# Audio tower on one core: projection folded behind its layer norm, a new order of all slots, and 20 products without use

## Chip, core and metric

The kernel runs on one core of a Trainium2 chip. The metric is the device time of one execution in microseconds (us). Matrix products run on TensorE (PE in the profile, its weight loads PEld), element-wise work on VectorE (DVE) and ScalarE (ACT), powers and most indirect transfers on GpSimd (POOL), loads on SyncE (SP).

## What is computed

64 signals of 4000 samples go through seven one-dimensional convolutions to 128 channels, each followed by a layer norm over the channels and an exact gelu. Twelve tokens a signal remain. They are normalised, projected to 192, and pass one attention layer and a feed-forward layer with nine experts:

```
for w, g, b, s in zip(conv_ws, ln_gs, ln_bs, strides):
    h = gelu(layernorm(conv1d(h, w, s), g, b))
norm_h = layernorm(h, fln_g, fln_b)
h = norm_h @ proj_w + proj_b
h = h + attention(layernorm(h))              # 6 heads of 32, softmax over 12 tokens
x = layernorm(h); p, routes = max, argmax of softmax(x @ Ws + bs)
out[e] = gelu(x @ W1[e] + b1[e]) @ W2[e] + b2[e]
h = h + (common = out[0], mixed with out[routes] by p)
```

All of it is float32. A 128x128 or wider product is two instructions in the trace ("x12" is six products).

## The kernel before

**Groups and chunks.** The 64 signals are eight groups (g = 0 to 7) of eight. A layer of a group is cut into chunks of up to four blocks of 128 columns; chunk (l, g, k) is cut k of layer l. There are 16 chunks a group, 128 in all. A chunk runs `conv` on TensorE, a square on ScalarE (L1371), a sum on VectorE (L1090), an addition and a power on GpSimd (L601, L604), a product with the result on VectorE (L1100), a `turn` (transposition) on TensorE (L772), and the gelu on ScalarE (L1389, L1400). Its transposition comes two slots after its convolution (`LAG`), so two other convolutions lie in between. A convolution also waits until the result of three chunks earlier has been read, and a transposition until the gelu of the chunk before has emptied the one bank that both use.

**Slots.** The order of everything is the list `SLOTS`: a head of 25 slots (`HEAD`, groups 0 and 1), bodies of 16 slots for groups 2 to 6, 18 slots `LAST` for group 7, and 34 slots `DRAIN`. A slot names one convolution chunk (or none), jobs, and preparations. Every engine goes through the slots in order and does its share of each. Jobs are: `raw`, `z`, `xt` (statistics and transposition of the samples), `l0` (layer 0: one product on TensorE, one gelu of 128x512 on ScalarE), and in the drain `up` and `down` of the common expert 0 (`down` i is six products of 128x192 for the 96 tokens of group i). A preparation `pow` is a power on GpSimd over 10 to 12 columns (L595), an `xs` scales samples on VectorE. After the head, jobs share two banks.

**Token runs.** When the last layer of group r is done, its 96 tokens go through run r (r = 0 to 7), a chain of small steps, whose slots come from the tables `STEP_AT` and `TIGHT`: `turn_h` transposes the tokens, `stat_h` and `power_h` make mean and rstd, `norm_h` (VectorE) normalises, `turn_norm_h` transposes back, `affine_h` (ScalarE) applies scale and offset, `project` multiplies by the 128x192 matrix, `stat_1` adds the bias and takes statistics, and then `power_1`, `norm_1`, `turn_1`, `qkv`, `scores`, `mask`, `less_max`, `exp` (ScalarE, which loads another function table for it and the gelu's again afterwards), `turn_probs`, `values`, `turn_heads`, `out_project`, `residual`, `norm_2`, `turn_2`, `logits`, `choose`, `rank`, `slot`, `scatter`. Run 7 has nothing but jobs beside it: in its slots TensorE also does `down` 4 (before `project`), `up` jobs and `down` 5 (between `turn_heads` and `out_project`).

**End.** After the last slot TensorE does `down` 6, six `up` jobs and `down` 7, waits for them, and then runs 13 tiles of 128 tokens sorted by expert (L991 to L1015).

## Time and profile before

| | |
|---|---|
| median of 3 runs | 624.17 us (621.41 to 624.65) |
| profiled execution, its own time | 617.57 us |
| its span, first to last instruction | 615.8 us |
| TensorE busy | 560.8 us, 91% |
| VectorE, ScalarE, GpSimd busy | 52%, 52%, 47% |
| mean granted TensorE clock | 0.971 |
| chain that ended last, by engine | TensorE 73%, GpSimd 8%, ScalarE 7%, VectorE 6%, issue 4% |

The profiled execution lies 1.8 us outside the span, and 6.6 us (1.1%) under the median of the other runs. The page cuts the span into 40 slices of 15.4 us; a digit is the busy share, or the granted clock, in tenths.

### The profile page before, as it was taken

Reading aid. Unit: us, or ns where it says so; the run is one execution under the profiler, and the core shown is the slowest. Engines: PE = TensorE matmul, PEld = TensorE weight load, DVE = VectorE, ACT = ScalarE, POOL = GpSimd, SP = SyncE. Lnnn points to the kernel's source line nnn. Section 1 sums busy time; section 2 is a strip of 40 time slices with the busy share of each in tenths; the row PEclk is TensorE's granted clock in tenths of the full one; section 3 lists DMA queues with packets and bytes.
Section 4 is the critical chain, followed back from the end, with each engine's and each line's share of the span. In section 5 each row is a group of like instructions: output and inputs, shape, how many; then the busy total and the mean of one; then the engine's idle time right before and its main releaser. Section 6 shows DMA issues by size and latency. Waiting matters only on the chain.

```text
span 615.8 us, 11336 instructions
## 1 busy us (share of the span) xinstructions
PE 560.8 (91%) x4195; PEld 524.1 (85%) x4195; DVE 319.6 (52%) x755; ACT 319.5 (52%) x507; POOL 290.7 (47%) x425
## 2 busy tenths in 40 slices
PE   6876899999999998999999999989999877789996
PEld 6675799988988998998999889988898765689995
DVE  4654356446476665755674766555554433342222
ACT  1645467555574656557465656664553413254441
POOL 5673276876339525842864495333333120114333
PEclk9998999999999999999999999999999976699999
DMA  6290000492000000000000000000000085041210
GB/s 185 59 300 11 2 1 10 117 241 53 2 1 1 15 2 1 1 6 0 3 1 6 1 2 6 1 1 0 6 3 5 1 238 135 5 129 54 58 37 11
DMA packets 17521, 26.36 MB, mean 43 GB/s; under 512 B 2172, under 2 KB 13397, under 8 KB 17467
## 3 DMA queue, kind: packets, MB, share of 16 engines
q1 hardware_dynamic: 14155, 15.85, 9.4%
q0 software_dynamic: 3296, 9.78, 6.2%
q8 instruction: 35, 0.57, 0.4%
q14 instruction: 19, 0.16, 0.1%
q10 hardware_dynamic: 16, 0.00, 0.0%
HBM read 17.13 MB, written 9.18 MB: 43 GB/s over the span
## 4 chain that ended last, share of the span: by engine, by line
PE 73%; POOL 8%; ACT 7%; DVE 6%; issue 4%; DMA 1%; SPq 1%; POOLq 0%; DVEq 0%; ACTq 0%
PE ps L760 18%; PE ps L752 9%; PE ps L749 7%; PE ps L772 5%; PE ps L1015 4%; POOL rstd L595 3%; PE ps L825 3%; PE ps L846 3%; PE ps L1004 3%; PE ps L1003 3%; POOL rstd L604 2%; ACT h L1400 2%; ACT work L1371 2%; PE ps L886 2%; PE ps L816 2%
## 5 line engine op out<-in xcount | busy, mean ns | idle before, releaser
L1371 ACT ACTIVATE work<-ps 128x512 f32<-128x512 f32 (+7 forms) x128 | 67.2, 525 | 182.4 <-PE ps L754 98.1
L760 PE MATMUL ps<-wt,wide 128*128 128x128 f32 (+2 forms) x1248 | 150.5, 274 | 5.9 <-ACT wide L1389 5.8
L760 PEld LDWEIGHTS ps<-wt,wide 128*128 128x128 f32 (+2 forms) x1248 | 144.6, 184 | 9.3 <-issue 6.5
L601 POOL TENSOR_TENSOR varv<-ssum,ceps 128x4 f32<-128x4 f32 (+7 forms) x128 | 26.0, 203 | 203.2 <-DVE ssum L1090 203.0
L604 POOL TENSOR_TENSOR rstd<-varv,neghalf 128x4 f32<-128x4 f32 (+7 forms) x128 | 116.8, 913 | 10.0
L1090 DVE TENSOR_REDUCE ssum<-work 128x4 f32<-128x512 f32 (+7 forms) x128 | 75.5, 590 | 85.3 <-ACT work L1371 85.2
L1100 DVE TENSOR_TENSOR work<-ps,rstd 128x512 f32<-128x512 f32 (+7 forms) x128 | 76.3, 596 | 82.8 <-POOL rstd L604 82.7
L1389 ACT ACTIVATE wide<-ps,lncol 128x512 f32<-128x512 f32 (+6 forms) x120 | 109.2, 910 | 2.6 <-PE ps L772 1.9
L595 POOL TENSOR_TENSOR rstd<-var,half 128x10 f32<-128x10 f32 (+2 forms) x39 | 83.6, 2151 | 8.9 <-DVE var L1056 8.9
L1400 ACT ACTIVATE h<-ps,lncol 128x512 f32<-128x512 f32 (+1 forms) x120 | 81.8, 725 | 2.1 <-PE ps L825 2.1
L752 PE MATMUL ps<-wt,h 128*128 128x256 f32 x304 | 76.1, 384 | 0.0
L772 PE MATMUL ps<-ident,work 128*128 128x128 f32 (+2 forms) x424 | 66.3, 270 | 6.8 <-ACT wide L1389 5.5
L749 PE MATMUL ps<-wt,h 128*128 128x128 f32 x416 | 57.0, 278 | 10.0 <-ACT h L1400 9.0
L749 PEld LDWEIGHTS ps<-wt,h 128*128 128x128 f32 x416 | 52.0, 193 | 11.8 <-issue 6.5
L752 PEld LDWEIGHTS ps<-wt,h 128*128 128x128 f32 x304 | 54.3, 194 | 5.2
L772 PEld LDWEIGHTS ps<-ident,work 128*128 128x128 f32 (+2 forms) x424 | 49.6, 142 | 9.7 <-issue 6.9
L825 PE MATMUL ps<-cols,w0t 120*128 120x512 f32 (+1 forms) x120 | 43.4, 424 | 2.1 <-DVE cols L1077 0.8
L1463 ACT ACTIVATE work<-ps 128x768 f32<-128x768 f32 x13 | 10.5, 811 | 34.1 <-PE ps L1004 34.1
L1015 PE MATMUL ps<-W2s,work 128*128 x156 | 27.3, 326 | 0.0
L708 POOL DMA_INDIRECT out_dram<-xnat,idt x13 | 13.1, 1011 | 29.5 <-DVE xnat L1328 28.9
L1077 DVE CAST cols<-ps 120x512 fp32r<-120x512 f32 (+1 forms) x40 | 25.1, 628 | 1.4 <-PE ps L816 1.3
L1015 PEld LDWEIGHTS ps<-W2s,work 128*128 128x128 f32 x156 | 25.1, 190 | 0.0
(224 smaller groups left out, 839.0 us busy)
## 6 DMA issues: line engine op xcount, KB each, us to landing
sorted_tokens<-zero POOLq DMA_DIRECT2D x1, 5886.5 KB, 30.0
W2s<-in_L_ffn_W_dram SPq DMA_DIRECT2D x9, 576.0 KB, 8.3
wide<-in_L_ffn_W_dram SPq DMA_DIRECT2D x8, 576.0 KB
cols<-sorted_tokens SPq DMA_DIRECT2D x13, 96.5 KB, 1.9
xnat<-in_x_dram SPq DMA_DIRECT2D x7, 135.0 KB
wt<-in_L_ffn_b_dram SPq DMA_DIRECT2D x1, 864.0 KB, 4.5
wide<-in_L_tok_conv_w_dram SPq DMA_DIRECT2D x4, 192.0 KB, 3.4
common_sums<-acc POOLq DMA_DIRECT2D x1, 579.0 KB, 6.3
```

What stands on the lines that cost most here:

```text
L595: gp.tensor_tensor(rstd0[:, lo:hi], var0[:, lo:hi], half0[:, lo:hi], ALU.pow).then_inc(s_pow, 1)
L604: gp.tensor_tensor(rstd[0:rows, idx, 0:count], varv[0:rows, idx, 0:count], neghalf[0:rows, 0:count], ALU.pow).then_inc(rstd_done, 1)
L749: nc.tensor.matmul(y[:, j * C:(j + 1) * C], local(2 * (lo + j) + 1), wt[:, 0, :], start=(j == 0), stop=False)
L752: nc.tensor.matmul(y[:, (j - 1) * C:(j + 1) * C], local(2 * (lo + j)), wt[:, 1:3, :].rearrange("p t c -> p (t c)"), start=False, stop=False)
L760: last = nc.tensor.matmul(y[0:rows, j * C:(j + 1) * C], h[l - 1][g % 2][:, at:at + rows], wt[:, TAP0[l] + tap, :], start=(tap == 0), stop= ...
L772: last = nc.tensor.transpose(tr[:, j * rows:(j + 1) * rows], xh[0:rows, n % 2, j * C:(j + 1) * C], ident[0:rows, 0:rows])
L1015: last = nc.tensor.matmul(o, ht[:, b, f * P:(f + 1) * P], W2s[:, bass.ds(own, 1), f, :].rearrange("p e d -> p (e d)"), start=(f == 0), sto ...
L1090: nc.vector.reduce_sum(ssum[0:rows, n % 4, 0:count], sq[0:rows, n % 2, 0:w].rearrange("p (j c) -> p j c", c=C), axis=X).then_inc(ssum_done, 1)
L1100: nc.vector.tensor_tensor(xh[0:rows, n % 2, 0:w].rearrange("p (j c) -> p j c", c=C), ybank(n)[0:rows, 0:w].rearrange("p (j c) -> p j c", c=C),
L1371: nc.scalar.activation(sq[0:rows, n % 2, 0:w], ybank(n)[0:rows, 0:w], ACT.Square).then_inc(sq_done, 1)
L1389: nc.scalar.activation(dst, src, ACT.Gelu, bias=lncol[:, 8 + l:9 + l], scale=lncol[:, l:l + 1]).then_inc(act_done, 1)
L1400: nc.scalar.activation(dst, src, ACT.Gelu, bias=lncol[:, 8:9], scale=lncol[:, 0:1]).then_inc(j_act, 1)
```

## The change

1. **Fold.** The final norm's scale and mean are put into the projection once: `projg` = centre times (scale times `projw`), and `projb` gets the offset's share. A run then projects the raw tokens and applies rstd together with the bias in one VectorE instruction. `norm_h`, `turn_norm_h` and `affine_h` are gone. Three new steps in slots 34 to 36 make the folded matrix.
2. **Epsilon in the sum.** The squares are written at a stride of 129, and the 129th element of each block holds 128 times epsilon, so the sum over 129 replaces sum and addition; the addition on GpSimd (L601) is gone from all 128 chunks.
3. **Order.** All slots are rewritten: head, body, last group, drain, and the tables of the runs (one each for runs 0, 1 to 4, 5, 6, 7).
4. **Products without use.** 20 products of 128x192 into a bank that nothing reads: in run 7 ahead of `turn_probs` (9), `values` (1), `turn_heads` (1) and `rank` (3), ahead of the first of the last six `up` jobs (4) and ahead of the first tile (2).

The core of the diff:

```diff
+BODY = [
+    ((1, 0, 0), [('xt', 0, 2)], []),
...
+    ((2, -1, 3), [('z', 1, 0), ('z', 1, 1)], [('pow', 1, 0), ('pow', 1, 1)]),
...
 HEAD = [
...
-    ((1, 0, 1), l0(0, 2, 0, 1) + [("raw", 1)], []),
-    (None, l0(0, 2, 2) + [("xt", 0, 3), ("z", 1, 0), ("z", 1, 1)], [("pow", 1, 0), ("pow", 1, 1)]),
-    ((1, 0, 2), l0(0, 3, 0, 1), []),
-    ((1, 0, 3), l0(0, 3, 2) + [("xt", 0, 4)], [("pow", 1, 2)]),
-    ((1, 0, 4), l0(0, 4, 0, 1, 2), [("pow", 1, 3), ("xs", 1, 0)]),
-    ((1, 0, 5), [("xt", 1, 0)], [("pow", 1, 4)]),
-    ((1, 0, 6), l0(1, 0, 0, 1, 2) + [("xt", 1, 1)], [("xs", 1, 1)]),
-    ((1, 1, 0), l0(1, 1, 0, 1, 2), []),
+    ((1, 0, 1), [('l0', 0, 2, 2), ('l0', 0, 2, 1), ('raw', 1), ('l0', 0, 2, 0), ('xt', 0, 3)], [('pow', 1, 0)]),
+    (None, [('z', 1, 0), ('z', 1, 1)], []),
+    ((1, 0, 2), [('l0', 0, 3, 0), ('l0', 0, 3, 1), ('l0', 0, 3, 2), ('xt', 0, 4)], [('pow', 1, 1), ('pow', 1, 2)]),
+    ((1, 0, 3), [('l0', 0, 4, 0), ('l0', 0, 4, 2), ('l0', 0, 4, 1)], [('pow', 1, 3), ('xs', 1, 0)]),
+    ((1, 0, 4), [], []),
+    ((1, 0, 5), [('xt', 1, 0)], []),
+    ((1, 0, 6), [('l0', 1, 0, 1), ('xt', 1, 1), ('l0', 1, 0, 2), ('l0', 1, 0, 0), ('l0', 1, 1, 1), ('l0', 1, 1, 0), ('l0', 1, 1, 2)], [('pow', 1, 4), ('xs', 1, 1)]),
+    ((1, 1, 0), [], []),
...
+BUSY = {"turn_probs": 9, "values": 1, "turn_heads": 1, "rank": 3, "last_up": 4, "tile": 2}
...
-                gp.tensor_tensor(varv[0:rows, idx, 0:count], ssum[0:rows, idx, 0:count], ceps[0:rows, 0:count],
-                                 ALU.add).then_inc(varv_done, 1)
...
+            def keep_busy(step):
+                for _ in range(BUSY.get(step, 0)):
+                    nc.tensor.matmul(ps[:, 0, 0:D], ident[:, :], W2s[:, 0, 0, :], start=True, stop=True)
...
+                if r == NT - 1:
+                    keep_busy(step)
+                if step == "fold":
...
+                    nc.tensor.matmul(pa[:, 0:D], centre[:, :], projg[:, :], start=True, stop=True).then_inc(t["fw"], 1)
...
-                if step == "turn_norm_h":
...
-                    nc.tensor.transpose(pb[:, 0:M], xn[:, 0:C], ident[0:M, 0:M]).then_inc(t["xhT"], 1)
...
+                    nc.tensor.matmul(pb[0:M, 0:D], h6[:, :], projg[:, :], start=True, stop=True).then_inc(t["pj"], 1)
...
-                if step == "norm_h":
-                    normed(xn[:, 0:C], pa[0:M, 0:C], "1", t["xh1"], r)
...
+                    ve.wait_ge(t["rs1"], r + 1)
...
+                    nc.vector.scalar_tensor_tensor(out=x1[:, :], in0=pb[0:M, 0:D], scalar=rs[:, 0:1], in1=projb[:, :],
+                                                   op0=ALU.mult, op1=ALU.add).then_inc(t["x1"], 1)
...
-                if step == "affine_h":
-                    ac.wait_ge(t["xhT"], r + 1)
-                    nc.scalar.activation(act[:, 0, :], pb[:, 0:M], ACT.Identity, bias=lncol[:, 15:16],
-                                         scale=lncol[:, 7:8]).then_inc(t["a1"], 1)
```

Where run 7 and its jobs stand, before and after (slots 141 to 156; a slot's jobs come before its steps):

```
before                                          after
141 down 3; logits(6)                           141 down 3; turn_2(6) logits(6)
142 turn (6,7,0); up 2.0                        142 turn (6,7,0); up 2.1; power_h
143 up 2.1; turn_h stat_h power_h norm_h        143 turn_h stat_h project stat_1 power_1
144 rank(6); turn_norm_h affine_h               144 up 2.0; rank(6); norm_1
145 down 4; project stat_1 power_1 norm_1       145 down 4, up 2.3; turn_1 copy_1 qkv split exp
146 up 2.2; turn_1 copy_1                       146 up 2.2, up 2.5
147 qkv split                                   147 scores mask; [9] turn_probs
148 up 2.3; scores mask less_max                148
149 up 2.4; exp                                 149 up 2.4; less_max sum_probs copy_probs
150 up 2.5; sum_probs turn_probs copy_probs     150
151 values divide                               151 [1] values divide residual norm_2
152 turn_heads copy_heads                       152 [1] turn_heads copy_heads out_project power_2
153 down 5; out_project residual norm_2         153
154 turn_2 copy_2                               154 down 5
155 logits choose                               155 turn_2 copy_2 logits choose slot
156 rank slot scatter                           156 [3] rank
```

A step stands at its engine's slot: an engine meets only its own steps, in order of slots. In the body `exp` moves from the slot after `scores` into the same slot, and the chunks of layer 2 run in the order 1, 2, 0, 3.

## Rows read from the trace of the kernel before

**Rows 1.** Page, part 2: granted TensorE clock in 40 slices.

```profile
PEclk9998999999999999999999999999999976699999
```

**Rows 2.** Windows: stretch, length, busy time of each engine, clock, DMA share, GB/s.

```profile
20.40:77.00 56.60, 45.80 (x304) 41.20 (x305) 26.40 (x51) 28.91 (x42) 25.30 (x28) 0.97 0.34 100
...
313.00:369.20 56.20, 54.49 (x436) 51.42 (x435) 35.61 (x81) 34.29 (x58) 31.60 (x45) 1.00 0.01 3
369.20:493.80 124.60, 117.81 (x911) 108.82 (x909) 66.16 (x158) 66.14 (x116) 42.63 (x82) 1.00 0.01 3
...
501.50:539.40 37.90, 28.85 (x125) 24.82 (x126) 12.78 (x44) 8.98 (x16) 3.42 (x6) 0.60 0.41 102
...
545.70:609.90 64.20, 63.39 (x494) 62.51 (x494) 17.06 (x53) 26.53 (x25) 26.17 (x27) 1.00 0.23 63
```

**Rows 3.** Waits of TensorE from 16 to 77 us: total us, times, longest.

```profile
PE ps L749 <- ACT h L1400: 9.0, 5, 2.7
```

**Rows 4.** Timeline of TensorE in the head: start, us, idle before and releaser.

```profile
53.38 1.43 PE L749 MATMUL ps<-wt,h 128*128 128x128 f32 x8 [2.19 <-ACT h L1400]
...
55.03 2.67 PE L752 MATMUL ps<-wt,h 128*128 128x256 f32 x6
```

**Rows 5.** Timeline of all engines, body of group 4, around `exp`.

```profile
284.81 0.75 DVE L1149 TENSOR_TENSOR t<-t,mx 96x576 f32<-96x576 f32 x1
...
286.27 1.28 ACT L1428 ACT_TABLE_LOAD   x1
...
287.57 0.68 ACT L1428 ACTIVATE t<-t 96x576 f32<-96x576 f32 x1
...
288.82 1.28 ACT L1389 ACT_TABLE_LOAD   x1
...
291.04 0.52 PE L772 MATMUL ps<-ident,work 128*128 128x128 f32 x3 [0.99 <-ACT wide L1389]
```

**Rows 6.** Timeline of TensorE from 462 us: runs 6 and 7 and the end.

```profile
474.52 1.52 PE L886 MATMUL ps<-act,watt 96*96 96x96 f32 x16
...
479.16 1.14 PE L894 MATMUL ps<-kpad,qs 96*96 96x288 f32 x4
...
495.74 0.29 PE L852 MATMUL ps<-ident,xn 96*96 96x96 f32 x1 [1.92 <-DVE xn L1114]
...
495.94 2.12 PE L846 MATMUL ps<-W2s,h 128*96 128x192 f32 x12
...
499.19 0.27 PE L864 MATMUL ps<-ident,h 128*96 128x128 f32 x1
...
502.36 4.05 PE L846 MATMUL ps<-W2s,h 128*96 128x192 f32 x12
...
509.42 0.29 PE L852 MATMUL ps<-ident,xn 96*96 96x96 f32 x1 [1.58 <-DVE xn L1114]
...
510.20 1.80 PE L886 MATMUL ps<-act,watt 96*96 96x96 f32 x16 [0.40 <-ACT act L1412]
...
514.22 2.21 PE L894 MATMUL ps<-kpad,qs 96*96 96x288 f32 x4
...
519.63 1.20 PE L900 MATMUL ps<-ident,t 96*96 96x96 f32 x6 [1.54 <-ACT t L1428]
...
521.74 2.13 PE L906 MATMUL ps<-vv,t 96*96 96x32 f32 x12 [0.91 <-DVE t L1159]
...
524.73 3.98 PE L846 MATMUL ps<-W2s,h 128*96 128x192 f32 x12
...
531.71 0.29 PE L852 MATMUL ps<-ident,xn 96*96 96x96 f32 x1 [2.35 <-DVE xn L1114]
...
534.49 0.49 PE L934 MATMUL ps<-hot,upper 96*96 96x9 f32 x2 [1.17 <-DVE hot L1187]
...
535.79 3.62 PE L846 MATMUL ps<-W2s,h 128*96 128x192 f32 x12
...
545.68 0.29 PE L991 MATMUL ps<-ident,cols 128*96 128x128 f32 x1 [0.49 <-issue]
```

More of the change, by code:

```diff
@@ L147, with of @@
+BODY = [
[16 rows of a table added]
+]
+def body(g):
+    def of(x):
+        return (x[0], g + x[1], *x[2:])
+    return [(c and (c[0], g + c[1], c[2]), [of(j) for j in jobs], [of(p) for p in prep]) for c, jobs, prep in BODY]
+HEAD = [
+    (None, [('raw', 0)], []),
+    (None, [('z', 0, 0), ('z', 0, 1)], [('pow', 0, 0), ('pow', 0, 1), ('pow', 0, 2), ('pow', 0, 3)]),
[15 rows of a table added]
+    ((1, 1, 2), [], [('pow', 2, 0)]),
[7 rows of a table added]
 ]
@@ L214 @@
+    (None, [('down', 5)], []),
     (None, [], []),
@@ L249 @@
-TIGHT = {"turn_h": 3, "stat_h": 3, "power_h": 3, "norm_h": 3, "turn_norm_h": 4, "affine_h": 4, "project": 5,
-         "stat_1": 5, "power_1": 5, "norm_1": 5, "turn_1": 6, "copy_1": 6, "qkv": 7, "split_queries": 7, "split_keys": 7,
-         "scores": 8, "mask": 8, "less_max": 8, "exp": 9, "sum_probs": 10, "turn_probs": 10, "copy_probs": 10,
-         "values": 11, "divide": 11, "turn_heads": 12, "copy_heads": 12, "out_project": 13, "residual": 13,
-         "power_2": 13, "norm_2": 13, "turn_2": 14, "copy_2": 14, "logits": 15, "choose": 15, "rank": 16, "slot": 16,
-         "scatter": 16}
@@ new lines @@
+STEPS = [[] for _ in SLOTS]
+RUN_0 = {'turn_h': 3, 'stat_h': 3, 'power_h': 3, 'project': 4, 'stat_1': 5, 'power_1': 4, 'norm_1': 7, 'turn_1': 8, 'copy_1': 8, 'qkv': 9, 'split_queries': 9, 'split_keys': 9, 'scores': 10, 'mask': 10, 'less_max': 10, 'exp': 10, 'sum_probs': 11, 'turn_probs': 12, 'copy_probs': 12, 'values': 13, 'divide': 13, 'turn_heads': 15, 'copy_heads': 15, 'out_project': 16, 'residual': 16, 'power_2': 16, 'norm_2': 17, 'turn_2': 18, 'copy_2': 18, 'logits': 19, 'choose': 19, 'rank': 20, 'slot': 20, 'scatter': 23, 'fold_weights': 0, 'fold': 1, 'fold_keep': 2}
@@ new lines @@
+RUN_1 = {'turn_h': 3, 'stat_h': 3, 'power_h': 3, 'project': 4, 'stat_1': 5, 'power_1': 4, 'norm_1': 7, 'turn_1': 8, 'copy_1': 8, 'qkv': 9, 'split_queries': 9, 'split_keys': 9, 'scores': 10, 'mask': 10, 'less_max': 10, 'exp': 10, 'sum_probs': 11, 'turn_probs': 12, 'copy_probs': 12, 'values': 13, 'divide': 13, 'turn_heads': 15, 'copy_heads': 15, 'out_project': 16, 'residual': 16, 'power_2': 16, 'norm_2': 17, 'turn_2': 18, 'copy_2': 18, 'logits': 19, 'choose': 19, 'rank': 20, 'slot': 20, 'scatter': 23}
@@ new lines @@
+RUN_5 = {'turn_h': 3, 'stat_h': 3, 'power_h': 3, 'project': 4, 'stat_1': 3, 'power_1': 4, 'norm_1': 5, 'turn_1': 6, 'copy_1': 6, 'qkv': 7, 'split_queries': 7, 'split_keys': 7, 'scores': 8, 'mask': 8, 'less_max': 8, 'exp': 9, 'sum_probs': 10, 'turn_probs': 10, 'copy_probs': 10, 'values': 11, 'divide': 11, 'turn_heads': 12, 'copy_heads': 12, 'out_project': 13, 'residual': 13, 'power_2': 13, 'norm_2': 13, 'turn_2': 14, 'copy_2': 14, 'logits': 15, 'choose': 15, 'rank': 17, 'slot': 17, 'scatter': 17}
```

240 lines of the change are left out of this document (107 added, 133 removed), and 28 rows, old and new, of tables (BODY, HEAD).

## The prediction

> **What bounds the kernel now.** I read the page first, then cut the span into windows. In the body of a group TensorE is busy for 54.5 of 56.2 us [rows 2]; the reader should see that VectorE has 35.6 and ScalarE 34.3 in the same stretch, so nothing but TensorE's own work and 1.7 us of idle time a group is to be had there. The 13 tiles at the end are the same: 63.4 busy of 64.2 us [rows 2]. Idle time lies in two other places. In the head TensorE is busy for 45.8 of 56.6 us [rows 2], and the waits say for what: five convolutions of layer 1 wait 9.0 us in all for gelus of layer 0 [rows 3]. In the last token run it is busy for 28.9 of 37.9 us, at a mean granted clock of 0.60 [rows 2]; the page shows this as 7, 6, 6 in the row of the clock [rows 1], which is time mostly at 1.2 instead of 2.4 GHz. Six products of `down` take 2.12 us at 495.9 and 4.05 us at 502.4 [rows 6]. Between them TensorE had stood idle for two stretches of some 2 us, the first of them shown at 495.74 [rows 6]. So the end of the drain is a serial chain at half speed, in which `down` 4 and `down` 5, which nobody waits for yet, stand in front of `project` and `out_project`.
>
> **The last run, step by step**, at full clock. Start: `down` 3 now comes before `turn_2`(6), into an idle time of 1.92 us that is there anyway [rows 6]; its two microseconds leave the chain, but the gelu of the last chunk has to be made first and limits the gain: 1.4 us. From `turn_h` (499.19) to `turn_1` (509.42) is 10.2 us [rows 6]. What remains is the transposition, 0.3, mean and rstd, and then add, statistics, power and norm. The last four took 2.35 us as the idle time before `turn_2` at 531.71 [rows 6], and mean and rstd alone are that without an add and a norm, an estimate of 1.5. The projection runs beside the power. Sum 4.1, a gain of 6.1. Behind `project` TensorE has `rank`(6), two `up` jobs and `down` 4, about 3.1 us, beside about as long a wait: they hide, and if they don't, a few tenths come back. From `turn_1` to `turn_probs` (509.42 to 519.63) is 10.2 us [rows 6]: 0.8 to `qkv` stays, the 20 instructions of `qkv` take 2.0 instead of 3.0 (the first 16 fall from 1.80 to 1.52, as at 474.52; that the other four, twice as wide, halve is an estimate), 1.0 to `scores` stays, `scores` fall from 2.21 to 1.14 as at 479.16, then 3.2 of mask, maximum, subtraction and exponential up to 519.63 [rows 6]. Sum 8.1, gain 2.1. The nine products without use stand in those 3.2 us: nine times a sixth of 2.12 less its overlap, 0.33 each, is 2.9 at full clock: they cost nothing, with 0.3 us to spare. From 519.63 to 524.73 is 5.1 [rows 6]. `up` 2.4 now stands ahead of `values` and needs a bank that a gelu after the exponential and a table load of 1.28 [rows 5] has to free; that, with one product without use, puts `values` at 2.4 instead of 2.1 behind `turn_probs`, and full clock takes 1.1 from the rest: gain 0.8. `down` 5 at 524.73, 3.98 us [rows 6], stood in the chain all but the 0.4 of a copy: gain 3.4. It goes into the 2.35 us before `turn_2`, where 2.0 fit. From 528.5 to 535.8, `out_project` to the end of `rank`, full clock gives 1.2, and three products (1.0) lie in the 1.17 before `rank` [rows 6]. Run 7 thus gains 1.4 + 6.1 + 2.1 + 0.8 + 3.4 + 1.2 = 15.0 us.
>
> **The end.** From 535.79 to the first tile at 545.68 TensorE is the bound: `down` 6, six `up`, `down` 7. `down` 6 falls from 3.62 to 2.12 [rows 6], and six products without use add 2.0 with nothing to hide them. Cost 0.4. What could be late next, the sorted tokens, need the routing chain on VectorE and a load; I bound this wait at nothing to 1 us, and take nothing, because TensorE reaches the first tile no earlier than before, counted from `rank`.
>
> **The head.** The `l0` jobs of quad 4 move from slot 9 to 8, those of quad 3 together to 7, those of group 1's quad 1 from slot 12 to 11: each gelu has one more convolution to hide behind. That answers to four of the five waits [rows 3]; the one at 53.38, 2.19 us [rows 4], is shortened only, since its three gelus are issued in the slot before. While the clock is low there, a convolution's six products of 256 columns take 2.67 us [rows 4], twice what they need at full clock; this goes too if TensorE stops idling. `pow` (1,0) and (1,1) are no longer back to back but (1,1) and (1,2) are, which moves a power on GpSimd from one chunk to the next. Bounds: nothing, if GpSimd's powers take the place of the gelus as the last wait (it is busy for 25.3 of 56.6 us, unevenly), and all 10.8 us of idle time [rows 2] plus 1.5 of clock. I take 8, nearer the upper end, because four waits each lose their cause. The epsilon in the sum takes an addition off GpSimd in each chunk, and adds one element in 129 to a sum on VectorE; it helps here and is hidden elsewhere.
>
> **The body.** A period has one wait of 0.99 at the transposition behind `exp`: ScalarE loads a table at 286.27, makes the exponential, loads the other at 288.82, and its gelu is late [rows 5]. The new order puts `exp` one slot earlier, right after the subtraction that ended at 285.56 [rows 5]; its first load then runs while VectorE still subtracts, so it comes 0.8 to 1.0 us earlier for TensorE. Behind it on ScalarE's queue wait a square and a gelu, which used to go first. Counting the next slots, the gelu ends some 0.2 us after TensorE arrives. Bounds: a loss of 2, if they now come late, and a gain of 1.7, the whole idle time. I take 0.7, for five runs 3.5 us. Runs 5 and 6 lie in a stretch with 6.8 us idle [rows 2], partly waits for `norm_h`, `rank` and the projection; the removed steps give 1.5. One transposition of 96 columns less in each run, some 0.1 us of TensorE, is 0.8 for all, and the fold's own two products and VectorE steps in slots 34 to 36 cost about the same: 0.
>
> **Table loads.** In the rows a load of 1.28 us at 286.27 is followed by the exponential at 287.57, so a switch costs ScalarE 1.30 [rows 5]. The Trainium skill, page "ScalarE: Activation LUTs", section "What ACT_TABLE_LOAD costs", counts 1.28 for the load and 1.38 more for draining, 2.66 a switch. By that figure, an estimate, the square and gelu queued behind `exp` would come 2.8 us later than I count in each of five runs, the body would lose 2.1 a run, and the total gain would be 14 us smaller. The rows decide for 1.30.
>
> **Sum.** 15.0 - 0.4 + 8 + 3.5 + 1.5 = 27.6, say 28 us. The profiled execution took 617.57 us, so its counterpart should take 589.6. The median is 6.6 us above it; I carry the gain over to it: 624.2 - 28 = 596. If the runs after the change are as fast as the profiled one was, the result lies up to 6 us lower.
>
> **Rivals.** *Forecast*, chance 0.62: 589 to 602 us. *Only the drain gains*, 0.18: in the head GpSimd's powers, and in the body the queue behind `exp`, take the place of the waits removed; for it speaks that a convolution also waits for the power of three chunks earlier, which a `pow` on GpSimd can hold up, against it that ScalarE ends four times as many waits. The gain is 15 to 19: 605 to 609. *The clock falls all the same*, 0.10: the chain has stretches in which only small transpositions and waits stand, and the products without use start late in it. Then they are 0.65 us each: nine take 5.9 in a gap of 3.2, three 2.0 in 1.2, `down` 4 and 5 outgrow their gaps by 1 and 1.5, and the six at the end cost 3 to 4. What is won by moving `down` and by the fold is paid back: run 7 ends about where it did, the end is 2 us later, and only head and body gain, 11 to 13: 611 to 613. *More than that*, 0.05: head and body lose all their idle time, 582 to 588. *Not faster*, 0.05: `exp` in the slot of `scores` stops ScalarE for the whole of mask, maximum and subtraction, 2.4 us, plus two loads, and the gelus behind it stall TensorE in every period. The drain and head gain 22.6, so this decides once it costs over 4.5 us in each of five periods, against the 0.99 of now; it is 624 if so, and up to 628. Against it: between `scores` and the transposition that would stall TensorE has 5.9 us of other work, by my count.
>
> **How the numbers follow.** The predicted time is the forecast's, 596. The range, 587 to 607, holds the forecast, most of the case in which only the drain gains, and some of the one beyond; it leaves out the low clock and the last case. About 0.5% (3 us) is what a measurement here can tell from no change. Faster: all cases but the last, 0.95, less a little for low clock together with a lost head, 0.94. Same 0.03, slower 0.03.
>
> **What would show it.** The clock's row reads 9 throughout the drain; run 7, from `turn_h` to `rank`, falls from 36 to about 22 us; `down` 4 and 5 have no step of the chain waiting behind them; the nine products end before `turn_probs` may start; TensorE's idle time in 20 to 77 us falls from 10.8 to 3 or 4; the wait of 0.99 in each period shrinks to 0.2; the tiles keep 64.2. I would be wrong if the clock fell in run 7, if waits for rstd (through VectorE's L1100) filled the head, or if a period of the body stayed at 56.2 us.

## The result

| | before | changed |
|---|---|---|
| median | 623.28 us (621.41 to 624.65) | 582.46 us (579.23 to 584.69) |
| ratio of the medians | | 0.9343, 95% interval 0.9281 to 0.9405 |
| profiled execution, its own time | 617.57 us | 580.36 us |
| its span | 615.8 us | 578.6 us |
| TensorE busy | 560.8 us, 91% | 552.7 us, 96% |
| mean granted clock | 0.971 | 0.992 |

(Both medians are of 4 runs; the prediction had 3 of the kernel before.) The change takes 40.8 us off the median, where 28 were predicted; 582.5 lies below the range, which began at 587. Of the 37.2 us that the spans differ, 8.1 are less busy time on TensorE and 29.1 are less idle time. The changed kernel ran in two more sets of six, beside experiments 10 and 12: 579.85 us (578.75 to 580.71) and 580.75 us (578.44 to 585.54), ratios 0.9314 (0.9278 to 0.9351) and 0.933 (0.929 to 0.937).

The page of the changed kernel: busy engines, part 2's row of the granted clock, the chain that ended last by engine, and from part 5 the power on GpSimd, before which no addition is left.

```profile
PE 552.7 (96%) x4231; PEld 521.0 (90%) x4231; DVE 317.9 (55%) x751; ACT 316.7 (55%) x499; POOL 264.8 (46%) x297
...
PEclk9999999999999999999999999999999989999999
...
PE 83%; POOL 7%; ACT 4%; DVE 3%; issue 1%; DMA 1%; SPq 1%; POOLq 0%; DVEq 0%; ACTq 0%
...
L605 POOL TENSOR_TENSOR rstd<-ssum,neghalf 128x4 f32<-128x4 f32 (+7 forms) x128 | 117.1, 915 | 194.2 <-DVE ssum L1101 194.0
```

Against [rows 1] the 7, 6, 6 of the drain has become an 8. Windows of the changed kernel, columns as in [rows 2]: the same head window, a period of the body, the last group with run 6, run 7, the end, and the tiles.

```profile
20.40:77.00 56.60, 54.79 (x401) 50.84 (x402) 33.52 (x67) 36.14 (x53) 30.40 (x22) 1.00 0.34 100
250.65:305.06 54.41, 53.77 (x434) 51.27 (x433) 35.28 (x79) 33.98 (x56) 28.11 (x28) 1.00 0.01 3
359.47:472.35 112.88, 110.69 (x862) 102.27 (x861) 59.80 (x142) 59.77 (x108) 34.88 (x48) 1.00 0.04 11
472.35:498.35 26.00, 23.23 (x143) 20.29 (x143) 10.64 (x33) 8.29 (x17) 3.17 (x7) 0.87 0.79 186
498.35:508.15 9.80, 9.36 (x64) 8.84 (x63) 7.35 (x34) 4.17 (x9) 0.96 (x1) 1.00 0.18 46
508.15:578.60 70.45, 63.67 (x495) 62.50 (x494) 17.48 (x53) 26.33 (x25) 27.48 (x28) 0.98 0.21 58
```

In the head TensorE was busy for 45.8 of these 56.6 us [rows 2]; now it is for 54.8. A body period is 54.4 us and has 0.6 idle. Run 7 went at a clock of 0.87, with part of it at 1.2 GHz.

The table below cuts each trace at the start of named TensorE instructions: the first convolution of layer 1 of group 0, of group 2, 3 and 7 (the stage "five periods" is group 2 to group 7), `turn_h` of run 7, the last product of its `rank`, the first tile, and the last instruction. It shows us, and in brackets the us at the low clock of 1.2 GHz inside the stage. The last microseconds of the tiles are at the low clock in every trace and have no bracket. The table comes from the starts in the trace and so is no row of a view.

```
kernel                      head        five periods   group 7   run 7        to tile     tiles   span
before                      82.3( 3.4)  275.5          120.3     36.4(27.6)   10.1(3.2)   70.2    615.8
changed                     70.6        267.6          112.9     26.0( 6.8)    9.8        70.5    578.6
changed, second set         71.7( 2.2)  267.6          112.9     25.1( 3.4)    9.8        70.1    579.0
changed, third set          71.9( 2.8)  268.0          112.9     25.0( 3.4)    9.8        70.4    580.2
no products                 70.6        267.3          112.9     26.7(11.0)   11.1(6.1)   70.3    580.0
no products, second set     71.8( 2.6)  267.4          112.9     27.3(13.6)   10.0(3.4)   70.3    581.7
fold, old order             85.4(10.3)  272.6          118.8     30.1(11.0)   11.1(6.1)   70.3    609.6
products alone              84.9(10.2)  275.5          120.3     37.0(20.4)   11.3(3.5)   70.3    620.4
old head                    83.1( 5.5)  267.2          112.9     26.3( 6.8)    9.8        70.3    592.2
exp later                   71.7( 2.2)  272.0          114.1     26.2( 6.8)    9.8        70.1    586.4
down in front               71.6( 2.1)  267.5          112.9     31.9(14.1)   11.0(2.9)   70.2    586.5
none at the end             71.7( 2.3)  267.6          112.9     24.0( 0.0)    9.8        70.2    577.5
addition back               71.0        273.5          113.7     26.2( 6.9)    9.8        70.1    585.3
ups first                   70.6        267.4          112.9     26.2( 6.8)   10.7(6.8)   70.4    579.2
ups first, no products      70.6        267.6          112.8     28.4(17.1)   10.7(6.8)   70.4    581.5
epsilon alone               86.3(12.0)  271.7          119.8     36.5(27.7)   10.0(3.0)   70.1    616.3
old last part               71.5( 2.0)  267.8          117.8( 3.4) 26.1( 6.8)  9.8        70.3    585.2
```

### The profile page after: what moved, and what is told of

Same layout as the page of the kernel before. It is cut to its first block, busy times and chain, and to the rows that moved or that the text cites. A ratio compares the mean times of both kernels' runs of the same rounds, so it can differ in the third digit from the quotient of the medians.

```text
span 578.6 us, 11288 instructions
## 1 busy us (share of the span) xinstructions
PE 552.7 (96%) x4231; PEld 521.0 (90%) x4231; DVE 317.9 (55%) x751; ACT 316.7 (55%) x499; POOL 264.8 (46%) x297
## 3 DMA queue, kind: packets, MB, share of 16 engines
q1 hardware_dynamic: 14155, 15.85, 10.3%
## 4 chain that ended last, share of the span: by engine, by line
PE 83%; POOL 7%; ACT 4%; DVE 3%; issue 1%; DMA 1%; SPq 1%; POOLq 0%; DVEq 0%; ACTq 0%
PE ps L761 23%; PE ps L753 9%; PE ps L773 7%; PE ps L750 7%; POOL rstd L599 5%; PE ps L1027 4%; PE ps L826 4%; PE ps L847 3%; PE ps L1016 3%; PE ps L1015 3%; PE ps L817 2%; PE ps L894 2%; PE ps L751 2%; PE ps L755 2%; PE ps L902 1%
## 5 line engine op out<-in xcount | busy, mean ns | idle before, releaser
L605 POOL TENSOR_TENSOR rstd<-ssum,neghalf 128x4 f32<-128x4 f32 (+7 forms) x128 | 117.1, 915 | 194.2 <-DVE ssum L1101 194.0
L1101 DVE TENSOR_REDUCE ssum<-work 128x4 f32<-128x516 f32 (+7 forms) x128 | 76.0, 594 | 69.6 <-ACT work L1390 69.1
L753 PE MATMUL ps<-wt,h 128*128 128x256 f32 x304 | 74.9, 380 | 0.0
L1479 ACT ACTIVATE work<-ps 128x768 f32<-128x768 f32 x13 | 10.6, 812 | 35.5 <-PE ps L1016 35.5
L610 POOL TENSOR_TENSOR veps<-mv,eps 96x1 f32<-96x1 f32 x24 | 5.5, 229 | 49.2 <-DVE mv L1120 49.1
L1330 DVE COPY xst<-ps 96x256 f32<-96x256 f32 x13 | 5.5, 420 | 37.3 <-issue 26.9
```

Of the source, the lines that this page charges most:

```text
L605: gp.tensor_tensor(rstd[0:rows, idx, 0:count], ssum[0:rows, idx, 0:count], neghalf[0:rows, 0:count], ALU.pow).then_inc(rstd_done, 1)
L753: nc.tensor.matmul(y[:, (j - 1) * C:(j + 1) * C], local(2 * (lo + j)), wt[:, 1:3, :].rearrange("p t c -> p (t c)"), start=False, stop=False)
L1101: nc.vector.reduce_sum(ssum[0:rows, n % 4, 0:count], sq[0:rows, n % 2, 0:count, :], axis=X).then_inc(ssum_done, 1)
```

## The experiments

Each is an edit of the changed kernel, unless it says of the kernel before. Ratios are to the kernel before on the same chip, with the 95% interval; the differences between the kernels of one chip are of medians. "Kernel 7" is the kernel of experiment 7, "none at the end" in the table.

**1. No products** (`k1_no_products`; repeated as `k14_no_products_again` beside the changed kernel).

```diff
-BUSY = {"turn_probs": 9, "values": 1, "turn_heads": 1, "rank": 3, "last_up": 4, "tile": 2}
+BUSY = {}
```

> The changed kernel without its 20 products. If the products hold the clock in the last token run: more stretches at half clock between 475 and 500 us, rank ends 3 to 8 us later than 498.4, total 583 to 590. If the moved work (down 4, down 5) already holds it: the clock's stretches stay at two, the end is 2 us earlier because the six products ahead of the last up jobs and the first tile are gone, total 579 to 582.

582.08 us (581.7 to 583.43), ratio 0.9374 (0.9305 to 0.9443). The first set of the changed kernel, 582.46, is another set with its own runs of the kernel before: by the medians the products cost 0.4 us, by the two ratios (0.9374 and 0.9343) they give some 1.9, and the intervals of the ratios overlap. So this says only that the products are worth little.

**2. Fold and epsilon in the old order, no products** (`k2_fold_old_order`). The slots and tables of before are kept, without the three removed steps, and with the three folding steps (lines against the changed kernel).

```diff
-PLACES = [RUN_0, RUN_1, RUN_1, RUN_1, RUN_1, RUN_5, RUN_6, RUN_7]
+STEP_AT = {"turn_h": 3, "stat_h": 3, "power_h": 3, "project": 6,
+           "stat_1": 6, "power_1": 6, "norm_1": 7, "turn_1": 8, "copy_1": 8, "qkv": 9, "split_queries": 9, "split_keys": 9,
...
+PLACES = [dict(STEP_AT, fold_weights=0, fold=1, fold_keep=2)] + [STEP_AT] * 4 + [TIGHT, dict(TIGHT, rank=18, slot=18, scatter=18), TIGHT]
```

> The kernel before with the fold and with epsilon in the sum, in the old order, without the products. If the order carries most of the gain: total 612 to 619, head within 2 us of before, a period of the body 55.9 to 56.1 us with the wait of 1.15 behind exp still there, the last run some 4 us shorter. If the fold and the shorter path to rstd carry much of it: head 4 us shorter or more, periods at 55 us, total under 608.

611.12 us (608.4 to 612.69), ratio 0.9827 (0.9749 to 0.9905), 11 us of the 40. Experiment 1 on the same chip has the same fold and epsilon and no products either, and took 582.08: the order is worth 29.0 us. Against before, run 7 is 6.4 us shorter and the five periods 2.9; the head is as long as in the other traces of the old head, 10.3 us of it at the low clock.

**3. Products alone, on the kernel before** (`k3_products_only`).

```diff
+BUSY = {"turn_probs": 9, "values": 1, "turn_heads": 1, "rank": 3, "last_up": 4, "tile": 2}
...
+                if r == NT - 1:
+                    keep_busy(step)
```

> The kernel before with nothing but the 20 products in its last run. If products alone hold the clock: low stretches in the last run shrink from 31 us to under 10, down 5 falls from 3.98 to 2.1, total 4 to 8 us lower, 614 to 618. If they come too late or too thin: clock as before, total 1 to 6 us higher.

623.65 us (616.82 to 627.84), ratio 1.0007 (0.9957 to 1.0058): nothing. Run 7 had 7 us less at the low clock than before, and was no shorter. Windows of this run 7 and of the changed kernel's without products (the second set):

```profile
501.79:538.78 36.99, 29.01 (x141) 25.85 (x140) 10.98 (x33) 9.23 (x18) 3.19 (x7) 0.72 0.53 119
```

```profile
474.10:501.39 27.29, 20.26 (x115) 17.13 (x115) 10.68 (x33) 8.36 (x17) 3.16 (x7) 0.75 0.71 179
```

At about the same mean clock, 0.72 and 0.75, one takes 37.0 us and the other 27.3; they differ in the fold, the order and the products. So it wasn't mainly the clock that made run 7 long.

**4. The old head** (`k4_old_head`): the 25 slots of `HEAD` as before, all else changed.

```diff
-    ((1, 0, 1), [('l0', 0, 2, 2), ('l0', 0, 2, 1), ('raw', 1), ('l0', 0, 2, 0), ('xt', 0, 3)], [('pow', 1, 0)]),
-    (None, [('z', 1, 0), ('z', 1, 1)], []),
...
+    ((1, 0, 1), l0(0, 2, 0, 1) + [("raw", 1)], []),
+    (None, l0(0, 2, 2) + [("xt", 0, 3), ("z", 1, 0), ("z", 1, 1)], [("pow", 1, 0), ("pow", 1, 1)]),
```

> The changed kernel with the head's 25 slots of before. If the gain of 11.6 us at the start of group 2 comes from the order of the gelus of layer 0: the five waits of 9 us come back, group 2 starts at 102 to 104 us, total 593 to 596. If it comes from the addition taken off GpSimd: group 2 starts at 94 to 98 us, total 585 to 590.

595.32 us (592.39 to 598.66), ratio 0.959 (0.9506 to 0.9673), 13.2 above the kernel without products on this chip. In the trace the head is 12.5 us longer than the changed kernel's, and no other stage moves by more than 0.4. The window of that head, from the first convolution of layer 1 to group 2:

```profile
22.59:105.69 83.10, 72.31 (x509) 67.08 (x508) 42.82 (x81) 45.00 (x68) 39.41 (x30) 0.97 0.24 70
```

**5. `exp` a slot later** (`k5_exp_later`), in runs 0 to 4, and `sum_probs` behind it (cut out of the long lines of the two tables).

```diff
-'exp': 10, 'sum_probs': 11
+'exp': 11, 'sum_probs': 12
```

> The changed kernel with exp of runs 0 to 4 back in the slot after scores (and the sum of the probabilities one slot later). If the slot of exp makes the body's gain: a wait of about 1 us comes back at the transposition behind it, periods grow from 54.4 to 55.4 to 55.8 us, total 5 us more, 586 to 589. If the order of the layer 2 chunks makes it: periods stay within 0.3 us of 54.4, total 581 to 584.

586.93 us (585.76 to 588.13), ratio 0.9472 (0.942 to 0.9523). In the trace the five periods are 4.4 us longer, and the stage of group 7, in which run 4 ends and run 5 begins, 1.2. The window of a period and, from the timeline of all engines, the two lines of the wait that came back:

```profile
254.97:310.44 55.47, 54.18 (x433) 51.27 (x432) 35.10 (x79) 34.10 (x57) 28.08 (x28) 1.00 0.01 3
```

```profile
277.31 1.28 ACT L1409 ACT_TABLE_LOAD   x1
...
279.42 0.52 PE L773 MATMUL ps<-ident,work 128*128 128x128 f32 x3 [0.59 <-ACT wide L1409]
```

**6. `down` in front of the chain again** (`k6_down_in_front`). In the drain `down` 4 goes to the slot before `project`, and `down` 5 ahead of `out_project`; `project` and `stat_1` go a slot later for it, `out_project` and its power too.

```diff
-    (None, [('up', 2, 0)], []),
-    (None, [('down', 4), ('up', 2, 3)], []),
+    (None, [('up', 2, 0), ('down', 4)], []),
+    (None, [('up', 2, 3)], []),
...
-    (None, [], []),
-    (None, [('down', 5)], []),
+    (None, [('down', 5)], []),
+    (None, [], []),
```

> The changed kernel with down 4 in front of the projection of run 7 and down 5 in front of out_project, as before the change. If their place in the chain is what made the last run long: turn_h to rank grows from 26.0 to 29.5 to 32 us, total 586 to 589. If the gain came only from the fold and from the clock: it grows by less than 2 us.

588.78 us (588.25 to 590.88), ratio 0.9519 (0.9465 to 0.9573). Run 7 takes 31.9 instead of 26.0 us. Timeline of TensorE in that run 7: the two `down` jobs, `project`, and the two waits behind them.

```profile
474.07 2.12 PE L847 MATMUL ps<-W2s,h 128*96 128x192 f32 x12
...
476.31 0.55 PE L883 MATMUL ps<-projg,h 128*96 128x192 f32 x2
...
479.64 0.29 PE L853 MATMUL ps<-ident,xn 96*96 96x96 f32 x1 [2.37 <-DVE xn L1124]
...
495.74 2.12 PE L847 MATMUL ps<-W2s,h 128*96 128x192 f32 x12
...
500.86 0.29 PE L853 MATMUL ps<-ident,xn 96*96 96x96 f32 x1 [2.35 <-DVE xn L1124]
```

Both `down` jobs went at the full clock, 2.12 us, and behind them stand waits of 2.4 us, the second just like the one in [rows 6]. Two jobs in front of two waits, instead of inside them, cost 5.9 us of run 7. The low clock has 7.3 us more of it than in the changed kernel, and by the rate found below some 1.9 of the 5.9 is that. The other 4.0 are the two waits: in kernel 7 they are 0.34 and 0.42 us instead of 2.37 and 2.35.

**7. No products at the end** (`k7_no_end_products`): the six behind `rank` left out, the 14 in run 7 kept.

```diff
-BUSY = {"turn_probs": 9, "values": 1, "turn_heads": 1, "rank": 3, "last_up": 4, "tile": 2}
+BUSY = {"turn_probs": 9, "values": 1, "turn_heads": 1, "rank": 3}
```

> The changed kernel with the 14 products in run 7, but without the 4 ahead of the last up jobs and the 2 ahead of the first tile. If these six only cost: rank to the first tile falls from 9.8 to 7.9 us, total 579 to 581. If they hold the clock there: it stays at 9.8 or grows towards the 11.1 us of the kernel without any product, total 582 to 584.

581.88 us (579.25 to 585.53), ratio 0.9416 (0.9347 to 0.9485). From the last product of `rank` to the first tile it is 9.81 us, with the six products 9.80. The timeline of TensorE there says what hid them:

```profile
497.57 2.17 PE L847 MATMUL ps<-W2s,h 128*96 128x192 f32 x12
499.58 0.36 PE L835 MATMUL ps<-xt,wide 96*128 96x96 f32 x2
...
501.47 0.46 PE L835 MATMUL ps<-xt,wide 96*128 96x96 f32 x2 [1.31 <-DVE h L1093]
...
507.30 0.28 PE L1003 MATMUL ps<-ident,cols 128*96 128x128 f32 x1 [0.49 <-issue]
```

The second `up` job needs the bank of `down` 6, which VectorE empties (L1093) only at the end of its queue of small routing steps. Windows of run 7 and the end in this kernel:

```profile
473.48:497.49 24.01, 20.48 (x142) 17.74 (x143) 10.47 (x33) 8.37 (x17) 3.16 (x7) 1.00 0.81 204
497.49:507.30 9.81, 7.58 (x52) 6.87 (x51) 7.36 (x34) 4.16 (x9) 0.96 (x1) 1.00 0.16 41
```

In this execution the clock never fell, so 24.0 us is run 7 at the full clock.

**8. The addition back** (`k8_addition_back`): GpSimd adds epsilon again, and the sum is over 128.

```diff
-                gp.tensor_tensor(rstd[0:rows, idx, 0:count], ssum[0:rows, idx, 0:count],
+                gp.tensor_tensor(varv[0:rows, idx, 0:count], ssum[0:rows, idx, 0:count], ceps[0:rows, 0:count],
+                                 ALU.add).then_inc(varv_done, 1)
+                gp.wait_ge(varv_done, n + 1)
+                gp.tensor_tensor(rstd[0:rows, idx, 0:count], varv[0:rows, idx, 0:count],
```

> The changed kernel with epsilon added again by GpSimd in each chunk. If the shorter path to rstd made part of the gain: head 1 to 3 us longer, periods up to 0.4 us longer, total 584 to 588. If it is hidden everywhere: every stage within 0.3 us, total 581 to 584.

587.18 us (587.07 to 591.12), ratio 0.9503 (0.944 to 0.9566). The prediction had 0 for it outside the head, and what I expected just before the run was up to 0.4 us a period. The five periods are 5.9 us longer in its trace, group 7 0.9 and the head 0.4. GpSimd's timeline in a period of the changed kernel:

```profile
280.36 4.50 POOL L599 TENSOR_TENSOR rstd<-var,half 128x12 f32<-128x12 f32 x2
284.82 1.01 POOL L605 TENSOR_TENSOR rstd<-ssum,neghalf 128x4 f32<-128x4 f32 x1
...
287.72 0.55 POOL L605 TENSOR_TENSOR rstd<-ssum,neghalf 104x1 f32<-104x1 f32 x1
...
291.25 1.01 POOL L605 TENSOR_TENSOR rstd<-ssum,neghalf 128x4 f32<-128x4 f32 x1
...
294.16 1.08 POOL L605 TENSOR_TENSOR rstd<-ssum,neghalf 128x4 f32<-128x4 f32 x1
```

and with the addition back:

```profile
284.35 4.50 POOL L602 TENSOR_TENSOR rstd<-var,half 128x12 f32<-128x12 f32 x2
288.81 0.20 POOL L608 TENSOR_TENSOR varv<-ssum,ceps 128x4 f32<-128x4 f32 x1
289.09 1.01 POOL L611 TENSOR_TENSOR rstd<-varv,neghalf 128x4 f32<-128x4 f32 x1
...
292.25 0.55 POOL L611 TENSOR_TENSOR rstd<-varv,neghalf 104x1 f32<-104x1 f32 x1
...
296.09 1.04 POOL L611 TENSOR_TENSOR rstd<-varv,neghalf 128x4 f32<-128x4 f32 x1
...
299.29 1.13 POOL L611 TENSOR_TENSOR rstd<-varv,neghalf 128x4 f32<-128x4 f32 x1
```

Neither shows an idle time in this stretch: GpSimd is behind. Counted from the start of the sample powers, the four powers start after 4.46, 7.36, 10.89 and 13.80 us, and with the addition after 4.74, 7.90, 11.74 and 14.94 us. An addition is 0.20 us and 0.28 until the power starts, and in a full queue the delays add up, to 1.1 us.

A period is 55.5 us instead of 54.4. Timeline of that stretch, the two places where TensorE now waits and VectorE's norm ahead of the second:

```profile
295.32 0.62 PE L823 MATMUL ps<-ident,xhl 128*120 128x128 f32 x4 [0.17 <-DVE xhl L1088]
...
295.88 0.38 DVE L1130 TENSOR_SCALAR xn<-acc,mv,rs 96x192 f32<-96x192 f32 x1 [0.71 <-POOL rs L618]
...
296.31 0.29 PE L859 MATMUL ps<-ident,xn 96*96 96x96 f32 x1 [0.37 <-DVE xn L1130]
```

The changed kernel has neither wait (its same transpositions start at 291.13 and 291.74), and neither is at a chunk's transposition. One is for scaled samples, which VectorE makes behind its late products with `rstd`; the other is for the norm of the token run, whose own power stands in GpSimd's full queue. Counted from the start of the period, TensorE is 0.4 us behind the changed kernel after the first, 0.7 after the second, and 1.1 after the first product of `rank`, which waits for VectorE too.

**9. The epsilon alone, on the kernel before** (`k10_epsilon_alone`).

```diff
-                gp.tensor_tensor(varv[0:rows, idx, 0:count], ssum[0:rows, idx, 0:count], ceps[0:rows, 0:count],
-                                 ALU.add).then_inc(varv_done, 1)
...
-                                     sq[0:rows, n % 2, 0:w].rearrange("p (j c) -> p j c", c=C), axis=X).then_inc(ssum_done, 1)
+                nc.vector.reduce_sum(ssum[0:rows, n % 4, 0:count], sq[0:rows, n % 2, 0:count, :], axis=X).then_inc(ssum_done, 1)
```

> The kernel before with epsilon in the sum and nothing else. If GpSimd's queue sets the pace in parts of the body in the old order too: periods 55.5 to 55.8 us, total 3 to 6 us lower than before. If the old order hides it: periods 56.0 to 56.2 us, head within 1 us, total within 2 us of before. With the kernel of fold and epsilon in the old order (11 us lower) it gives the fold alone: 5 to 8, or 9 to 11.

615.55 us (613.58 to 618.08), ratio 0.9892 (0.9851 to 0.9934). In the five periods of the old order it gives 3.8 us; taken out of the new one it costs 5.9. The old head got no shorter by it (86.3 us, 12.0 of them at the low clock). Experiment 2 has the fold besides: run 7 is another 6.4 us shorter there, the five periods are 0.9 longer, and the ratios, 0.9827 against 0.9892, put the fold by itself at some 4 us.

**10. Ups first** (`k9_ups_first`), on kernel 7: the six `up` jobs go ahead of `down` 6, and VectorE empties `down` 6 and `down` 7 together behind its routing steps. **11. The same without any product** (`k11_ups_first_no_products`), and **the changed kernel again** beside both (`k12_changed_again`).

```diff
-AFTER = [('down', 6), ('up', 3, 0), ('up', 3, 1), ('up', 3, 2), ('up', 3, 3), ('up', 3, 4), ('up', 3, 5), ('down', 7)]
+AFTER = [('up', 3, 0), ('up', 3, 1), ('up', 3, 2), ('up', 3, 3), ('up', 3, 4), ('up', 3, 5), ('down', 6), ('down', 7)]
```

> The changed kernel without the six products at the end, and with the last six up jobs ahead of down 6; VectorE takes down 6 and 7 right after the shares. Theory: rank to the first tile (9.8 us with and without the six products) is set by VectorE, which empties the bank of down 6 only after the routing chain, so the second up job waits for it and the six products lie in that wait. Then this distance falls to 7.8 to 8.6 us, total 580 to 581. If the arrival of the sorted tokens or of the weights sets it, it stays at 9.5 or more.

> As the kernel with the up jobs first, but without any product without use. If the 14 products of the last run are worth something once the end is no longer bound by VectorE: 1 to 3 us slower than that kernel. If not: within 1 us of it.

> The changed kernel again, on the same chip as the three others: 580 to 584.

Ups first: 578.56 us (577.96 to 580.97), ratio 0.9295 (0.9258 to 0.9331). Without products: 583.58 us (582.03 to 584.66), 0.9379 (0.9341 to 0.9416). The changed kernel: 579.85 us. Ups first is the fastest kernel measured, but its runs overlap those of the changed kernel, and the trace doesn't settle it: its profiled execution had 6.8 us at the low clock on the way to the tile, and took 10.7 us for it instead of 9.8. It does show that the wait for VectorE is gone: TensorE waits for nothing there but 0.5 us of issue before the tile, and the rest is its own work. The runs with and without products don't overlap: in this pair the 14 products are worth 5.0 us. The two profiled executions differ by 2.3 us only; that of ups first was the slowest of its seven. Run 7 of the kernel without any, window:

```profile
472.02:500.43 28.41, 21.73 (x115) 18.41 (x115) 10.76 (x33) 8.28 (x17) 3.16 (x7) 0.70 0.69 171
```

**12. The old last part** (`k13_old_last`): `LAST` and `DRAIN` up to slot 140 with the chunks and jobs in the old order, runs as changed; beside it the two repeats, without products (`k14_no_products_again`) and the changed kernel (`k15_changed_third`).

```diff
-    ((2, 6, 2), [('l0', 7, 2, 0)], []),
-    ((2, 6, 0), [('xt', 7, 3), ('l0', 7, 2, 2)], []),
-    ((2, 6, 1), [('l0', 7, 3, 0), ('l0', 7, 3, 2)], []),
...
+    ((2, G7 - 1, 0), l0(G7, 2, 2), []),
+    ((2, G7 - 1, 1), [("xt", G7, 3)], []),
+    ((2, G7 - 1, 2), l0(G7, 3, 0, 1), []),
```

> The changed kernel with the chunks and jobs of slots 107 to 140 in the old order; the tables of the token runs stay new. If the order of chunks and jobs makes the gain there: from the start of group 7 to the last run 117 to 119 us instead of 112.9, total 584 to 587. If the shorter token runs (no norm_h, no turn_norm_h, exp and qkv earlier) make it: 113 to 114.5 us, total within 2 us of the changed kernel.

> The changed kernel without its 20 products, beside the changed kernel on the same chip. If the products keep the clock: 2 to 4 us slower than the changed kernel in the medians. If they do nothing: within 1 us.

> The changed kernel once more, as the partner of the two others on one chip: 579 to 584.

Old last part: 586.45 us (583.88 to 588.8), ratio 0.9417 (0.9376 to 0.9457), against 580.75 (578.44 to 585.54) for the changed kernel. Its stage of group 7 takes 117.8 us instead of 112.9, 3.4 of them at the low clock. Without products: 582.76 us (581.35 to 585.63), 0.9369 (0.9336 to 0.9403); its runs overlap those of the changed kernel.

## Why the prediction was wrong

The forecast of 596 was 13.5 us too high. 9.2 of it are the sum, which made 589.6 of the profiled execution where it was 580.4; the other 4.3 came in when it was carried to the median. The median fell where the rival "more than that" had it (582 to 588, chance 0.05), and its condition, that head and body lose all their idle time, nearly holds: of 10.8 us in the window of the head 1.8 are left, of 1.7 in a period 0.6. By stages, gain in us of the spans:

```
stage                      predicted   profiled   at full clock
head                          8          11.8
five periods                  3.5         7.8
group 7 and run 6 (with the
  start of run 7)             2.9         7.4
run 7, turn_h to rank        13.6        10.4        12.4
to the tile                  -0.4         0.2
tiles                         0          -0.3
sum                          27.6        37.2
```

(The stages add up to 37.4; 0.2 were lost ahead of the first convolution.)

**Failed step 1: the epsilon "helps here and is hidden elsewhere", counted as 0.** This is the largest piece that was counted as nothing. With the addition back, the stages from the head to run 7 are 7.4 us longer, and the median is 4.7 above the changed kernel's and 5.3 above kernel 7's on the same chip. The prediction gave no row for it, and the page of before, with GpSimd busy for 47%, looks like room. It also had the places the wrong way round: the head loses 0.4 us with the addition back, the five periods 5.9. Experiment 8 shows that much of a period's load stands in one stretch of some 15 us that begins with the sample powers, in which GpSimd has no idle time. There every addition delays what is queued behind it, and what reaches TensorE is the delay of a preparation and of the token run.

**Failed step 2: `exp` at 0.7 us a period.** The wait of 0.99 [rows 5] was to shrink to 0.2. It went away. Timeline of the changed kernel, ScalarE with its two loads, the subtraction on VectorE, the transposition behind them, and the only wait left in the period:

```profile
267.60 1.28 ACT L1444 ACT_TABLE_LOAD   x1
...
268.22 0.75 DVE L1168 TENSOR_TENSOR t<-t,mx 96x576 f32<-96x576 f32 x1
...
269.00 0.69 ACT L1444 ACTIVATE t<-t 96x576 f32<-96x576 f32 x1
...
270.08 1.28 ACT L1409 ACT_TABLE_LOAD   x1
...
271.38 0.70 ACT L1409 ACTIVATE wide<-ps,lncol 128x416 f32<-128x416 f32 x1
...
272.22 0.52 PE L773 MATMUL ps<-ident,work 128*128 128x128 f32 x3
...
283.50 0.66 PE L761 MATMUL ps<-wt,wide 128*104 128x128 f32 x4 [0.63 <-ACT wide L1409]
```

The first load runs while VectorE still subtracts, as the prediction said, and the transposition at 272.22 has no wait. Putting `exp` back costs 5.6 us (4.4 and 1.2 in the two stages), where 3.5 were counted for it. So the mechanism was right, and the size was 1.1 us a period and not 0.7. A period as a whole lost 1.7 or 1.8 us, from 56.2 [rows 2] to 54.4: 1.1 of idle time, and 0.7 of the busy column. One transposition less is some 0.1 of that. Another 0.4 goes with the waits and not with the work: in a period of the kernels of experiments 5 and 8 TensorE has the 433 instructions that it has in the changed kernel's, and its busy column is 54.2 instead of 53.8. The rest I can't put to an instruction.

Gains of one stage don't add. In the five periods and group 7 together the later `exp` costs 5.6 us, the addition 6.8 and the old order of the last part 4.9, which makes 17.3, and the whole change gained 15.2 there. In the old order the epsilon alone gives 3.8 in the five periods (experiment 9), and taken out of the new order it costs 5.9: that fits one late engine covering part of another's lateness, so that all of it is seen only when both are early, but no run shows this by itself. What the new order of layer 2's chunks does by itself was not tried.

**Failed step 3: the runs 5 and 6, at 1.5 us.** The stage of group 7 gained 7.4. I had 6.8 us of idle time before me [rows 2] and priced only the steps that went away. Experiment 12 puts 4.9 of the 7.4 down to the order of the chunks and jobs in the last part, and 5 and 8 put 1.2 to `exp` and 0.9 to the addition. Part of the 4.9 is the clock: with the old order it fell for 3.4 us in a stretch in which TensorE was idle for 2.0 of 13.5, as this window of kernel 12 shows.

```profile
446.56:460.08 13.52, 11.52 (x78) 10.61 (x77) 4.79 (x13) 2.63 (x6) 3.71 (x7) 0.87 0.02 6
```

**The head: mechanism right, size 8 where it is 12.** The waits of convolutions for gelus of layer 0 went, all but 0.2 us, also the one at 53.38 that was to be shortened only. What is left of waits for these gelus is mostly at layer 0's own products. The waits of TensorE from 16 to 77 us in the changed kernel, where [rows 3] had 9.0 us:

```profile
PE ps L826 <- ACT h L1420: 1.6, 2, 0.8
...
PE ps L750 <- ACT h L1420: 0.2, 1, 0.2
```

GpSimd did not take their place, so the rival in which only the drain gains fell: putting back the old head (experiment 4) costs 12.5 us, and putting `exp` back (experiment 5) 5.6, where that rival has nothing for either. 8 was short because I kept the wait at 53.38 in part and took less than the bound of all 10.8 us of idle time. The 1.5 for the clock fits the profiled execution: experiment 3 has the same head as before, 6.8 us more of it at 1.2 GHz, and is 2.6 us longer there, so the 3.4 us of before are worth some 1.3 by this estimate. For other executions it was little: the old head was at 1.2 GHz for 3.4 to 12.0 us in five traces.

**Run 7: held at the full clock.** 13.6 was predicted from `turn_h` to `rank`, and 12.4 were gained at the full clock. The removed layer norm, and the two `down` jobs inside waits of the chain, did it: `turn_h` to `turn_1` took 4.48 us at the full clock in kernel 7 where the prediction built 4.1, and `turn_1` to `turn_probs` 8.34 where it built 8.1. Experiment 6 loses 5.9 again by moving the two jobs and their neighbours.

What did not hold is the clock. "The clock's row reads 9 throughout the drain" is wrong: it fell in the changed kernel too. Timeline of TensorE:

```profile
474.02 3.71 PE L847 MATMUL ps<-W2s,h 128*96 128x192 f32 x12
...
482.93 3.09 PE L858 MATMUL ps<-W2s,ident 128*128 128x192 f32 x18
486.29 0.70 PE L908 MATMUL ps<-ident,t 96*96 96x96 f32 x6 [0.27 <-ACT t L1444]
...
492.53 2.96 PE L847 MATMUL ps<-W2s,h 128*96 128x192 f32 x12
```

The prediction had named a fall in run 7 as a sign of being wrong. `down` 4 took 3.71 us and `down` 5 2.96, against 2.17 and 2.12 in kernel 7; the 18 instructions without use took 3.09 at full speed and were over 0.27 us before `turn_probs` could start, as counted. The rival that rests on this fall (611 to 613) came true in its condition and was wrong in its price of some 15 us. In the traces with the new order of the drain (experiment 6 left aside), run 7 took 24.0, 25.0, 26.0, 26.7, 27.3 and 28.4 us with 0, 3.4, 6.8, 11.0, 13.6 and 17.1 us at the low clock: a quarter of a microsecond for each. In the chain that is left, TensorE's own products are the smaller part, some 9 of the 24.0 us (an estimate from kernel 7's timeline); the rest is the way over VectorE, GpSimd and ScalarE. Their busy time in run 7 stays nearly the same whether the granted clock there is 1.00, 0.87 or 0.70: VectorE 10.5, 10.6 and 10.8 us, ScalarE 8.4, 8.3 and 8.3, GpSimd 3.2 each time. The slow jobs of [rows 6] made the clock look like the cause; it was that they stood in the chain.

**The products.** On the kernel before they give nothing. In the new order, again without experiment 6, the time at the low clock in run 7 was 11.0 to 17.1 us without them and 0 to 6.8 with, which by the rate above is worth 1 to 4 us. The three comparisons of medians give -0.4 (two sets), 2.0 (overlapping runs) and 5.0 us (separate runs). So they help, by something between nothing and 5 us; the size isn't settled.

**The end.** A loss of 0.4 was forecast and a gain of 0.2 measured, and the reason was wrong: the six products are hidden by a wait of 1.31 us for VectorE that the prediction did not see. They cost nothing, and `down` 6 took 2.17 us as predicted.

**Failed step 4: carrying the gain to the median.** The median of before lay 6.6 us above its profiled run, and I added that to the result. The changed kernel's median is 2.1 above its own. The prediction named this ("the result lies up to 6 us lower") and left it out of its sum and of its range. Such a distance is in good part the luck of the one execution that is profiled: in the two later sets of the changed kernel the median is 0.9 and 1.2 us below the profiled run, and with the old head it is 1.5 and 1.3 above (experiments 3 and 4) or 0.2 and 2.5 below (2 and 9). The profiled run of before was a fast one of its kernel: its head has 3.4 us at the low clock, the other four traces of the old head 5.5, 10.2, 10.3 and 12.0, the new head 0 to 2.8. What the slower executions lost by the clock could be gained too, and the median gained 40.8 us where the spans gained 37.2. That these 3.6 us are the clock in the head fits the traces and was not shown.

**Two readings that changed nothing.** The two idle stretches of some 2 us are not both between the two `down` jobs: the one at 495.74 lies ahead of the first. And the 2.67 us at 55.03 [rows 4] are six instructions, three products; at the full clock they take 1.46 us.

**Table loads.** The second load at 270.08 is followed by its gelu at 271.38, and the first at 267.60 by `exp` at 269.00, which waited for the subtraction until 268.97. From the start of a load to an activation that waits for nothing else it is 1.30 us here too, not the 2.66 of the Trainium skill (page "ScalarE: Activation LUTs", section "What ACT_TABLE_LOAD costs"). The measurement decides.

## What to carry to other kernels

An engine at 47% busy can still set the pace: look at its queue around its longest instruction, and price an operation removed there by what is queued behind it, not by its share; then follow the delay to the instruction that the bounding engine waits for, which here was no chunk's. Where a job that nobody waits for stands in a serial chain, put it inside one of the chain's waits; moving two such jobs out again cost 5.9 us of run 7, where the products without use gave between nothing and 5, and with the jobs inside a microsecond at the low clock cost a quarter of one. A distance between one profiled run and the median is partly luck; look at how the clock of the other executions differs before carrying it over.
